# Gated cross-attention block on one core: input norm two batches ahead, gate and up products one step earlier, final sum ahead of a clip, six whole feed-forward row blocks

## The chip, the cores and the metric

The kernel runs on one core of a Trainium2 chip. The metric is the device time of one execution in microseconds. It is written in Bass: every engine has its own instruction stream in program order, and engines wait for each other by semaphores. The engines are TensorE (PE), VectorE (DVE), ScalarE (ACT), GpSimd (POOL), and SyncE (SP), whose queue issues most DMA transfers.

## The reference, cut to what matters

32 batches; per batch x is 100 x 256, the context 1444 x 256, 16 heads of 16, and a hidden width of 704.

```python
h = layernorm(x)                               # "input norm"
q, k, v = h @ Wq.T + bq, ctx @ Wk.T + bk, ctx @ Wv.T + bv
probs = softmax(where(mask, clip(q @ k.T / 4, -50, 50), -10000 -> -50))
delta = layernorm(rs * ((probs @ v) @ Wo.T + bo)) * gamma + beta
x1 = x + tanh(g_xattn) * delta
z = layernorm(x1)                              # then quantised per row to 8 bits
hid = silu(z @ w1.T) * (z @ w2.T)              # gate and up products, ternary weights
out = x1 + tanh(g_ffn) * (quant(hid) @ w3.T)   # "final sum"
```

## The kernel before, in words

Each batch's 1444 context rows are cut into 12 tiles of 121 rows (the last 113) and 3 chunks of 4 tiles. Three batches are in work at once. While the scores and exponentials of batch b run through their 12 steps (n = 0 to 11), the same loop body also does the k and v projections and the input norm and query of batch b+1 (called `c` in the code), the output projection, second norm and gate and up products of batch b-1 (`d`), and the hidden row's quantisation, the down product and the final sum of batch b-2. The order on every engine is written out by hand: each engine has a function `batch` with one `for n in range(NT)` and `if n == ...` lines. Nothing is scheduled by a tool.

In a step TensorE does: 4 score products (`scores`, L1192), half a projection item (`ctx_item`: 3 products of L1233 for k, or 6 of L1247 for v), whatever small product the step has, 4 more score products and the other half item. At n = 1, 5 and 9 it also does the probability times v products of four tiles (`pv`, L1212, 128 records). ScalarE takes each half tile of scores through the exponential (L549, 24 in a batch), copies projections out of PSUM (L561, L570) and copies the results of the small products. VectorE clips each exponentiated tile (`clip`, L783), splits the context into a high and a low part (`split_head` L744, `split_rest` L750), makes the low part of k (`k_rest`, L774), and does the softmax division and both norms. GpSimd makes the small reciprocal roots of the norms and issues the 12 transfers of the stacked query (`stack_q`, L475). SP issues three times 12 transfers of stacked k (`stack_k`, L305) in a batch, and the loads.

The places that the change and the prediction touch:

- All small products share one PSUM bank, `mb`, so each must be read out before the next is written. The output projection (`delta`, L1280, in step 3) writes `mb` after the down product (`down`, L1313, in step 2) has been read by the final sum (`result`, L957 on VectorE), and so it waits for `result_done`:

```python
def delta(b, older):
    pe.wait_ge(dve_post, D_V.after(b, "oT"))
    if older:
        pe.wait_ge(result_done, b.n)
```

- The other waits of TensorE on VectorE that are spoken of: `v_item` (L1247) waits for `k_rest` of the item whose PSUM bank it takes over (`k_lo_done`), `pv` waits for `clip_done`, `x_turn` (L1264) for `xn` and `dl`, `h_turn` (L1306) for `hq`. `scores` waits for the exponential two half tiles before, and at the start of a chunk for its 12 stacked transfers.
- VectorE's steps 1 to 3 before: `split_head`, `k_rest`, `clip`, `split_rest`, `attention_read` and `sums_inverse` (L844 to L855); then `k_rest`, `attention_out`, `clip`, `result`, `x_stats`; then `x_aggr`, `clip`, `x_norm`, `delta_out` (L869). In step 0 it ends the hidden row of batch b-2: `hidden_gate` (L925), `clip`, `hidden_up` (L931), `h_max` (L935), `h_scale`, `h_round`, `h_quant`.
- The input norm is `x_stats`, `x_aggr` (VectorE), `x_rstd_of` (GpSimd, L431 and L433) and `x_norm` (VectorE, L803, waits for GpSimd).
- The gate and up products (`up`, L1298) come in halves of 352 columns: gate 0 and up 0 in step 9, gate 1 in step 10, up 1 in step 11. ScalarE reads each gate half twice (`ffn_gate`, L617 and L618) and each up half once (`ffn_up`, L623).
- The hidden row of 704 is turned in six blocks (`h_turn`), five of 128 columns and one of 64, and read by two activations (`h_turned`, L610 and L611).

A second pass over all batches with `base` set, which guards against infinities, follows under a condition that these inputs don't meet; it is in the program and doesn't run.

Of the kernel before, what the change touches and what calls it, by code (L numbers as in the profile page):

```python
# [41 lines left out]
def flamingo_block(nc, x, ctxT, maskT, g_xattn, g_ffn, wqT, bq, wkT, bk, wvT, bv, woT, bo,  # L42
# [25 lines left out]
    P = 128  # L68
# [37 lines left out]
    with es:  # L106
# [69 lines left out]
        hq = sb("hq", [S, F], bf16)  # L176
# [54 lines left out]
        D_A = Steps("x2T", "t0", "g0", "u0", "t1", "g1", "u1", "hTa", "hTb")  # L231
# [166 lines left out]
        def _(pool):  # L398

            nc.gpsimd.memset(e_sb[2][:, (FT - 1) * H:FT * H], 0.0)  # L400
            nc.gpsimd.memset(e_sb[3][0:TT, (NT - 1) * NB:NT * NB], 0.0).then_inc(s_setp, 1)
# [78 lines left out]
            def batch(b, nxt, prev):  # L480
                for n in range(NT):
                    if n == 3:
                        if nxt:
                            x_rstd_of(b.plus(1))
                            mask_of(b.plus(1))
# [8 lines left out]
                    if n == 11 and nxt:  # L494
                        residual(b.plus(1), prev)

# [19 lines left out]
            def passes(base):  # L516
# [4 lines left out]
                residual(whole(0, base), False)  # L521
                batch(whole(0, base), True, False)
                if base:
                    with pool.Fori(base // 2, (base + NB - 2) // 2) as i:
                        batch(Batch(2 * i + 1, i, 1, base), True, True)
                        batch(Batch(2 * i + 2, i + 1, 0, base), True, True)
                else:
                    for n in range(1, NB - 1):
                        batch(whole(n), True, True)
                batch(whole(NB - 1, base), False, True)  # L530
# [8 lines left out]
        def _(act):  # L539
# [67 lines left out]
            def h_turned(b):  # L607
                act.wait_ge(pe_post, D_T.after(b, "hT"))
                v = mb16[:, 0:FT * S].rearrange("p (k s) -> p k s", k=FT)
                nc.scalar.activation(hT[:, 0:FT - 1, :], v[:, 0:FT - 1, :], ACT.Copy).then_inc(act_post, 1)  # L610
                nc.scalar.activation(hT[0:FL, FT - 1, :], v[0:FL, FT - 1, :], ACT.Copy).then_inc(act_post, 1)  # L611
# [66 lines left out]
        def _(dve):  # L678
# [268 lines left out]
            def h_quant(b):  # L947
                d_wait(b, "hround")
                dv(V.tensor_scalar(hq[:, :], th[:, :], MAGIC, QMAX, ALU.subtract, ALU.min))
# [17 lines left out]
            def batch(b, nxt, prev, prev2):  # L967
# [3 lines left out]
                for n in range(NT):  # L971
# [483 lines left out]
```

## Time and profile before

| | us |
|---|---|
| median of 3 runs (lowest, highest) | 1438.97 (1438.78, 1439.39) |
| the profiled execution's own time | 1438.62 |
| its span, first to last instruction | 1436.8 |
| busy: PE, DVE, ACT, POOL | 1348.5, 1131.2, 965.1, 469.7 |
| busy share: PE, DVE, ACT, POOL | 94%, 79%, 67%, 33% |
| chain that ended last: PE, DVE, ACT, issue | 52%, 25%, 13%, 7% |

The span has three parts: a start of some 70 us (weights, and the projections of the first batch), 31 batches that follow each other in the loop, and an end of some 40 us in which the last batches' remaining work runs one thing after another. Small waits repeat once in each batch, so a wait of half a microsecond stands for some 15 us of the time. "Idle before" of an engine says what ended the idle time; a weight load (PEld) runs ahead of its product, so a wait shows on PEld, on PE, or on both.

### The profile page before, as it was taken

The page shows a single profiled execution, that of the slowest core. Times are in us where ns is not written, and L with a number is a line of the kernel's source. Part 1 is how long each engine was busy: PE and PEld are TensorE (multiplying, and loading weights), DVE is VectorE, ACT ScalarE, POOL GpSimd, SP SyncE. Part 2 cuts the span into 40 slices and gives each one's busy share as a digit, 9 for nine tenths or more (in the row PEclk, how much of TensorE's full clock was granted, in tenths as well). Part 3 has the DMA queues.
Part 4 walks back from the last instruction along what each step waited for, and adds up shares of the span by engine and source line. Part 5 has one row for each costly group of instructions (what it writes and reads, how often), then busy time and mean ns, then how long its engine had stood idle before and what let it go on. Part 6 is the DMA issues. An engine that isn't in the chain of part 4 may idle for free.

```text
span 1436.8 us, 48034 instructions
## 1 busy us (share of the span) xinstructions
PE 1348.5 (94%) x19984; PEld 1220.3 (85%) x19984; DVE 1131.2 (79%) x2241; ACT 965.1 (67%) x1634; POOL 469.7 (33%) x759
## 2 busy tenths in 40 slices
PE   5699999999999999999999999999999999999982
PEld 5599888888988888898888898888889888888971
DVE  6668788878878887877887887888788788878763
ACT  2367776676776767777676777767777767676751
POOL 3523333233333223233323333332333332232310
PEclk9699999999999999999999999999999999999995
DMA  7467666666766666776667676666667666766620
GB/s 217 110 160 174 157 153 156 164 158 167 169 163 155 154 163 166 168 169 156 156 152 171 161 176 160 158 150 161 163 162 173 158 157 155 167 163 162 139 52 8
DMA packets 142477, 222.13 MB, mean 155 GB/s; under 512 B 29162, under 2 KB 135598, under 8 KB 142254
## 3 DMA queue, kind: packets, MB, share of 16 engines
q1 hardware_dynamic: 129966, 199.31, 57.7%
q0 software_dynamic: 12288, 19.69, 6.2%
q8 instruction: 160, 2.62, 0.8%
q14 instruction: 63, 0.52, 0.1%
HBM read 54.00 MB, written 3.28 MB: 40 GB/s over the span
## 4 chain that ended last, share of the span: by engine, by line
PE 52%; DVE 25%; ACT 13%; issue 7%; POOL 2%; SPq 1%; DMA 0%; DVEq 0%; POOLq 0%; ACTq 0%
PE pvb L1212 13%; PE sc L1192 12%; PE cb L1233 11%; PE cb L1247 9%; ACT e_sb L549 7%; DVE e_sb L783 4%; DVE zt L855 3%; DVE c_lo L750 2%; PE mb L1280 2%; PE mb L1271 2%; DVE tiny L935 2%; PE mb L1298 2%; DVE k_lo L774 2%; DVE th L945 1%; ACT us L623 1%
## 5 line engine op out<-in xcount | busy, mean ns | idle before, releaser
L549 ACT ACTIVATE e_sb<-sc 121x800 f32<-121x800 f32 (+1 forms) x768 | 644.8, 844 | 201.4 <-PE sc L1192 191.3
L1192 PE MATMUL sc<-q_st,k_st 96*121 96x200 f32 (+1 forms) x3072 | 476.4, 278 | 7.1 <-DMA q_st<-bd_hi 3.1
L1192 PEld LDWEIGHTS sc<-q_st,k_st 96*121 96x121 f32 (+1 forms) x3072 | 416.3, 186 | 42.5 <-issue 9.0
L783 DVE TENSOR_SCALAR e_sb<-e_sb,hi_b 121x1600 f32<-121x1600 f32 (+1 forms) x384 | 399.4, 1047 | 38.3 <-ACT e_sb L549 38.1
L1212 PE MATMUL pvb<-e_sb,v_sb 121*32 121x100 f32 x12288 | 286.2, 251 | 0.1
L1212 PEld LDWEIGHTS pvb<-e_sb,v_sb 121*32 121x32 f32 x12288 | 264.7, 110 | 22.6 <-issue 19.0
L774 DVE SCALAR_TENSOR_TENSOR k_lo<-cb,bk_c,k_hi 128x484 fp32r<-128x484 f32 (+1 forms) x192 | 134.4, 700 | 137.8 <-ACT k_hi L561 137.8
L1247 PE MATMUL cb<-wv_hi,c_hi 128*121 128x256 f32 (+1 forms) x768 | 227.8, 297 | 15.2 <-DVE k_lo L774 12.2
L475 POOL DMA_DIRECT2D q_st<-bd_hi x256 | 183.2, 719 | 107.9 <-DVE bd_lo L829 104.7
L1247 PE MATMUL cb<-wv_hi,c_lo 128*121 128x256 f32 (+1 forms) x768 | 217.0, 283 | 0.0
L1247 PE MATMUL cb<-wv_lo,c_hi 128*121 128x256 f32 (+1 forms) x768 | 216.9, 282 | 0.0
L431 POOL TENSOR_SCALAR x_ve<-mv 100x1 f32<-100x1 f32 x32 | 24.9, 777 | 560.1 <-DVE mv L799 560.1
L1247 PEld LDWEIGHTS cb<-wv_hi,c_hi 128*121 128x121 f32 (+1 forms) x768 | 142.3, 185 | 26.0 <-DVE k_lo L774 25.2
L1233 PE MATMUL cb<-c_hi,wk_hi 128*128 128x484 f32 (+1 forms) x384 | 154.1, 401 | 0.0
L1233 PE MATMUL cb<-c_hi,wk_lo 128*128 128x484 f32 (+1 forms) x384 | 147.2, 383 | 0.0
L1233 PE MATMUL cb<-c_lo,wk_hi 128*128 128x484 f32 (+1 forms) x384 | 147.0, 383 | 0.0
L1247 PEld LDWEIGHTS cb<-wv_hi,c_lo 128*121 128x121 f32 (+1 forms) x768 | 141.8, 185 | 0.1
L1247 PEld LDWEIGHTS cb<-wv_lo,c_hi 128*121 128x121 f32 (+1 forms) x768 | 141.0, 184 | 0.0
L561 ACT ACTIVATE k_hi<-cb,bk_c 128x484 fp32r<-128x484 f32 (+1 forms) x192 | 126.3, 658 | 4.8 <-PE cb L1233 4.8
L750 DVE TENSOR_TENSOR c_lo<-c_in,c_hi 128x968 fp32r<-128x968 f32 (+1 forms) x96 | 112.4, 1171 | 0.0
L570 ACT ACTIVATE v_sb<-cb 121x512 f32<-121x512 f32 x160 | 97.1, 607 | 21.0 <-PE cb L1247 21.0
L623 ACT ACTIVATE us<-mb,tiny 100x352 f32<-100x352 f32 x64 | 36.6, 572 | 78.0 <-PE mb L1298 78.0
(139 smaller groups left out, 1609.0 us busy)
## 6 DMA issues: line engine op xcount, KB each, us to landing
k_st<-k_hi SPq DMA_DIRECT2D x512, 121.0 KB, 2.8
c_in<-in_ctxT SPq DMA_DIRECT2D x64, 484.0 KB, 3.8
k_st<-k_lo SPq DMA_DIRECT2D x256, 121.0 KB, 2.9
k_st<-k_hi SPq DMA_DIRECT2D x256, 119.0 KB, 2.3
c_in<-in_ctxT SPq DMA_DIRECT2D x32, 476.0 KB, 3.6
k_st<-k_lo SPq DMA_DIRECT2D x128, 119.0 KB, 2.4
q_st<-bd_hi POOLq DMA_DIRECT2D x256, 50.0 KB, 3.3
q_st<-bd_lo POOLq DMA_DIRECT2D x128, 50.0 KB, 3.2
```

What stands on the lines that cost most here:

```text
L475: nc.gpsimd.dma_start(q_st[b.par][QR * part:QR * (part + 1), :, j, :].bitcast(f32), src[QR * j:QR * (j + 1), :, :, :].rearrange("p k a s - ...
L549: nc.scalar.activation(e_sb[e_slot(b, n)][0:TL[n], k * SW:(k + 1) * SW].rearrange("p (o c) -> p o c", o=2), sc[q % NSC][0:TL[n], :, 0:2 * PW],
L561: nc.scalar.activation(k_hi[slot][:, o, 0:CL[u]], cb[o][:, 0:CL[u]], ACT.Identity, bias=bk_c[:, o:o + 1]).then_inc(k_hi_done, 1)
L570: nc.scalar.activation(v_sb[0:TL[n], n:n + 2, :, 0:4:3, :].rearrange("p n q a d -> p (n q) a d"), cb[i][0:TL[n], :].rearrange("p (q a d) - ...
L623: nc.scalar.activation(us[:, cols], mb[0:S, 0:FH], ACT.Copy, scale=tiny[:, 5:6]).then_inc(act_post, 1)
L750: V.tensor_tensor(c_lo[slot][:, :, 0:w], c_in[slot][:, :, 0:w], c_hi[slot][:, :, 0:w].bitcast(f32), ALU.subtract).then_inc(split_done, 1)
L774: V.scalar_tensor_tensor(k_lo[slot][:, o, 0:w], cb[o][:, 0:w], bk_c[:, o:o + 1], k_hi[slot][:, o, 0:w].bitcast(f32), ALU.add, ALU.subtract ...
L783: V.tensor_scalar(e, e, E_LO, hi_b[b.par][0:TL[n], n:n + 1], ALU.max, ALU.min).then_inc(clip_done, 1)
L1192: last = T_.matmul(sc[q % NSC][0:TL[n], e // 2, (e % 2) * PW:(e % 2 + 1) * PW], k_st[st_slot(b, n // TPC)][:, pr // NQ, pr % NQ, t0:t0 + T ...
L1212: last = T_.matmul(pvb[QR * j:QR * (j + 1), col:col + S], v_sb[0:TL[n], n, pr, 2 * a:2 * a + 2, :].rearrange("p x d -> p (x d)"), e[0:TL[n ...
L1233: last = T_.matmul(cb[o][:, 0:w], wt[:, k, o * P:(o + 1) * P], ct[slot][:, k, 0:w], start=i == 0, stop=i == 5)
L1247: last = T_.matmul(cb[i][0:TL[n], half * H:(half + 1) * H], ct[slot][:, k, t0:t0 + TL[n]], wt[:, k, :], start=(k == 0 and a == 0), stop=(k ...
```

## The change

1. **Input norm two batches ahead.** `x_stats` and `x_aggr` of batch b+2 stand at the end of step 9 of batch b, `x_norm` at the head of step 11, and GpSimd's `x_rstd_of(b+2)` at its step 11 behind `stack_q` and `residual`; before they were for batch b+1 in steps 2 and 3. The second batch's norm is made before the loop starts. `split_rest` of the first chunk moves from step 1 to step 2, behind the clip.
2. **Gate and up products one step to the front.** Gate 0 in step 8, up 0 and gate 1 in step 9 (ahead of and behind `pv`), up 1 in step 10; the reads on ScalarE and VectorE move with them, and `h_max` stands at the end of step 11, where it was in step 0 of the next batch.
3. **Final sum ahead of a clip.** `result` stands before the clip in step 2.
4. **Six whole blocks.** `hq` is widened to 768 columns, the last 64 set to zero once, so that `h_turn`, `h_turned` and `down` treat six blocks of 128, and one activation reads them.

```diff
-        hq = sb("hq", [S, F], bf16)
+        hq = sb("hq", [S, FT * P], bf16)
@@ GpSimd, setup and batch
+            nc.gpsimd.memset(hq[:, F:FT * P], 0.0)
...
                     if n == 3:
                         if nxt:
-                            x_rstd_of(b.plus(1))
                             mask_of(b.plus(1))
...
                     if n == 11 and nxt:
                         residual(b.plus(1), prev)
+                        if nxt2:
+                            x_rstd_of(b.plus(2))
@@ ScalarE
-                nc.scalar.activation(hT[:, 0:FT - 1, :], v[:, 0:FT - 1, :], ACT.Copy).then_inc(act_post, 1)
-                nc.scalar.activation(hT[0:FL, FT - 1, :], v[0:FL, FT - 1, :], ACT.Copy).then_inc(act_post, 1)
+                nc.scalar.activation(hT[:, :, :], mb16[:, 0:FT * S].rearrange("p (k s) -> p k s", k=FT), ACT.Copy
+                                     ).then_inc(act_post, 1)
...
-                    if prev and n in (9, 10):
-                        ffn_gate(d, n - 9)
-                    if prev and n in (9, 11):
-                        ffn_up(d, (n - 9) // 2)
+                        ffn_up(d, n - 9)
+                    if prev and n in (8, 9):
+                        ffn_gate(d, n - 8)
@@ VectorE, batch
-                    if nxt:
-                        if n == 3:
-                            x_aggr(c)
-                        if n == 6:
-                            q_head(c)
-                    if prev2 and n == 0:
-                        hidden_gate(b.plus(-2), 1)
+                    if nxt and n == 6:
+                        q_head(c)
                     if prev:
                         if n == 2:
                             attention_out(d)
-                        if n == 10:
-                            hidden_gate(d, 0)
+                        if n in (9, 10):
+                            hidden_gate(d, n - 9)
+                    if nxt2 and n == 11:
+                        x_norm(b.plus(2))
+                    if prev2 and n == 2:
+                        result(b.plus(-2))
                     if n:
                         clip(b, n - 1)
...
-                    if nxt and n % 4 == 1:
+                    if nxt and n in (2, 5, 9):
                         split_rest(c, n // 4)
...
                     if prev2 and n == 0:
-                        hidden_up(b.plus(-2), 1)
-                        for step in (h_max, h_scale, h_round, h_quant):
+                        for step in (h_scale, h_round, h_quant):
                             step(b.plus(-2))
-                    if prev2 and n == 2:
-                        result(b.plus(-2))
-                    if nxt and n == 2:
-                        x_stats(c)
-                    if nxt and n == 3:
-                        x_norm(c)
+                    if nxt2 and n == 9:
+                        x_stats(b.plus(2))
+                        x_aggr(b.plus(2))
...
-                        if n == 10:
-                            hidden_up(d, 0)
+                        if n in (9, 10):
+                            hidden_up(d, n - 9)
+                        if n == 11:
+                            h_max(d)
@@ TensorE, batch
+                        if n == 8:
+                            up(d, 0, 0)
                         if n in (9, 10):
-                            up(d, n - 9, 0)
-                        if n == 11:
-                            up(d, 1, 1)
+                            up(d, n - 9, 1)
                     attend()
...
                     if prev and n == 9:
-                        up(d, 0, 1)
+                        up(d, 1, 0)
```

How the order moves, at three places. First VectorE in steps 1 to 3. The names: `e_sb` is a tile of exponentials, `oT` and `zt` the attention output and the row sums, `y_out` the final sum, `mb` the shared PSUM bank. Before:

```order
L783 TENSOR_SCALAR e_sb<-e_sb,hi_b 121x1600
L750 TENSOR_TENSOR c_lo<-c_in,c_hi 128x968
L844 TENSOR_SCALAR oT<-pvb,submask 128x200
...
L855 RECIPROCAL zt<-zt 128x200
L774 SCALAR_TENSOR_TENSOR k_lo,watch<-cb,bk_c,k_hi 128x476
L859 TENSOR_TENSOR oT<-oT,zt 128x200
L783 TENSOR_SCALAR e_sb<-e_sb,hi_b 121x1600
L957 SCALAR_TENSOR_TENSOR y_out<-mb,tiny,x 100x256
L794 BN_STATS stat<-x_in 100x6
```

With the change:

```order
L787 TENSOR_SCALAR e_sb<-e_sb,hi_b 121x1600
L848 TENSOR_SCALAR oT<-pvb,submask 128x200
...
L859 RECIPROCAL zt<-zt 128x200
L778 SCALAR_TENSOR_TENSOR k_lo,watch<-cb,bk_c,k_hi 128x476
L863 TENSOR_TENSOR oT<-oT,zt 128x200
L961 SCALAR_TENSOR_TENSOR y_out<-mb,tiny,x 100x256
L787 TENSOR_SCALAR e_sb<-e_sb,hi_b 121x1600
L754 TENSOR_TENSOR c_lo<-c_in,c_hi 128x968
```

The low part of the context no longer stands between the clip and the reading of the attention sums, the final sum stands ahead of the second clip, and the input norm's statistics are gone from here.

Second TensorE in steps 8 and 9 (`w12q` are the gate and up weights). Before:

```order
L1233 MATMUL cb<-c_hi,wk_lo 128x484
L1298 MATMUL mb<-w12q,x2T 100x352 x2
L1212 MATMUL pvb<-e_sb,v_sb 32x100 x64
L1298 MATMUL mb<-w12q,x2T 100x352 x2
L1192 MATMUL sc<-q_st,k_st 121x200 x4
```

With the change:

```order
L1237 MATMUL cb<-c_hi,wk_lo 128x484
L1302 MATMUL mb<-w12q,x2T 100x352 x2
L1196 MATMUL sc<-q_st,k_st 121x200 x4
...
L1302 MATMUL mb<-w12q,x2T 100x352 x2
L1216 MATMUL pvb<-e_sb,v_sb 32x100 x64
L1302 MATMUL mb<-w12q,x2T 100x352 x2
L1196 MATMUL sc<-q_st,k_st 121x200 x4
```

The pairs ahead of and behind the `pv` products are now up 0 and gate 1; gate 0 stands a step ahead of them, step 10 has up 1, and step 11 has none.

Third VectorE in steps 9 to 0 (`th`, `gs` and `us` are the hidden row's halves, `stat` and `mv` the input norm's statistics). Before:

```order
L750 TENSOR_TENSOR c_lo<-c_in,c_hi 128x2x476
L774 SCALAR_TENSOR_TENSOR k_lo,watch<-cb,bk_c,k_hi 128x484
L925 SCALAR_TENSOR_TENSOR th<-th,gs 100x352
L783 TENSOR_SCALAR e_sb<-e_sb,hi_b 121x1600
L931 TENSOR_TENSOR gs<-th,us 100x352
L783 TENSOR_SCALAR e_sb<-e_sb,hi_b 121x1600
L925 SCALAR_TENSOR_TENSOR th<-th,gs 100x352
L783 TENSOR_SCALAR e_sb<-e_sb,hi_b 113x1600
L931 TENSOR_TENSOR gs<-th,us 100x352
L935 TENSOR_REDUCE tiny<-gs 100x1
L939 TENSOR_SCALAR tiny<-tiny 100x1
```

With the change:

```order
L754 TENSOR_TENSOR c_lo<-c_in,c_hi 128x2x476
L798 BN_STATS stat<-x_in 100x6
L803 BN_AGGR mv<-stat 100x2
L935 TENSOR_TENSOR gs<-th,us 100x352
L778 SCALAR_TENSOR_TENSOR k_lo,watch<-cb,bk_c,k_hi 128x484
L929 SCALAR_TENSOR_TENSOR th<-th,gs 100x352
L787 TENSOR_SCALAR e_sb<-e_sb,hi_b 121x1600
L935 TENSOR_TENSOR gs<-th,us 100x352
L807 TENSOR_SCALAR xn<-x_in,mv,x_rstd 100x256
L787 TENSOR_SCALAR e_sb<-e_sb,hi_b 121x1600
L939 TENSOR_REDUCE tiny<-gs 100x1
L787 TENSOR_SCALAR e_sb<-e_sb,hi_b 113x1600
```

The hidden row's second half and its maximum come ahead of the clip of tile 11, and `xn`, which waits for GpSimd, now has the clips of tiles 10 and 11 behind it. On GpSimd the order of the instructions is the same as before (`x_res`, `x_ve`, `x_rstd`, `hi_b`, `d_ve`); only the batch whose norm they make is one later.

## Rows read from the trace of the kernel before

**Rows 1.** The page, its first line.
```profile
span 1436.8 us, 48034 instructions
```

**Rows 2.** Windows of two batches: us; PE, PEld, DVE, ACT, POOL busy; PEclk, DMA, GB/s.
```profile
91.30:131.64 40.34, 39.79 (x614) 36.55 (x613) 31.35 (x61) 29.35 (x50) 13.63 (x23) 1.00 0.71 171
723.34:765.53 42.19, 41.28 (x626) 37.58 (x625) 34.41 (x69) 29.99 (x52) 13.99 (x23) 1.00 0.68 157
```

**Rows 3.** Who waited for whom, whole run: engine, line, releaser; us, times, longest.
```profile
PEld mb L1280 <- issue: 26.9, 29, 0.9
...
PE mb L1280 <- DVE y_out L957: 21.7, 29, 0.8
...
PEld cb L1247 <- DVE k_lo L774: 25.2, 58, 9.9
...
PE mb L1306 <- DVE hq L949: 6.4, 2, 3.7
```

**Rows 4.** Chain of waits from 734 to 740 us: start, us, what.
```profile
735.41 0.96 DVE e_sb L783
...
736.38 0.41 DVE y_out L957
```

**Rows 5.** Timeline of TensorE, same batch: start, us, engine, line, operation, count, idle before.
```profile
726.67 2.96 PE L1212 MATMUL pvb<-e_sb,v_sb 121*32 121x100 f32 x128
...
732.36 0.95 PE L1313 MATMUL mb<-w3q,hT 128*100 128x256 bf16 x6
...
735.88 0.28 PE L1247 MATMUL cb<-wv_lo,c_hi 128*121 128x256 f32 x1
...
736.92 1.08 PE L1280 MATMUL mb<-wo,oT 128*100 128x256 f32 x4 [0.75 <-DVE y_out L957]
```

**Rows 6.** Timeline of VectorE, same batch.
```profile
725.45 0.89 DVE L935 TENSOR_REDUCE tiny<-gs 100x1 f32<-100x704 f32 x1
...
730.11 1.16 DVE L750 TENSOR_TENSOR c_lo<-c_in,c_hi 128x968 fp32r<-128x968 f32 x1
...
731.18 0.42 DVE L844 TENSOR_SCALAR oT<-pvb,submask 128x200 f32<-128x200 f32 x1
...
734.51 0.62 DVE L774 SCALAR_TENSOR_TENSOR k_lo<-cb,bk_c,k_hi 128x476 fp32r<-128x476 f32 x1
...
736.29 0.48 DVE L957 SCALAR_TENSOR_TENSOR y_out<-mb,tiny,x 100x256 f32<-100x256 f32 x1
...
739.46 0.42 DVE L869 SCALAR_TENSOR_TENSOR dl<-mb,bo_t 100x256 f32<-100x256 f32 x1
...
749.57 0.72 DVE L774 SCALAR_TENSOR_TENSOR k_lo<-cb,bk_c,k_hi 128x484 fp32r<-128x484 f32 x1
```

**Rows 7.** Timeline of ScalarE, same batch, steps 10 and 11.
```profile
762.87 0.84 ACT L549 ACTIVATE e_sb<-sc 121x800 f32<-121x800 f32 x1
...
764.78 0.59 ACT L623 ACTIVATE us<-mb,tiny 100x352 f32<-100x352 f32 x1
```

**Rows 8.** Timeline of GpSimd, same batch.
```profile
760.56 0.75 POOL L439 TENSOR_TENSOR x_res<-x_in,beta_t 100x256 f32<-100x256 f32 x1
```

**Rows 9.** Groups by line and shape, GpSimd: busy us, mean ns, idle before.
```profile
L446 POOL TENSOR_SCALAR d_ve<-dmv,scal 100x1 f32<-100x1 f32 x32 | 43.9, 1371 | 97.2 <-DVE dmv L879 97.2
```

**Rows 10.** Timeline of the SP queue, same batch, with the landing of such a transfer.
```profile
751.98 1.99 SPq L305 DMA_DIRECT2D k_st<-k_hi  x2
...
762.17 0.70 SPq L305 DMA_DIRECT2D k_st<-k_lo  x1
```

**Rows 11.** The page, DMA issues: count, KB each, median us to landing.
```profile
k_st<-k_lo SPq DMA_DIRECT2D x256, 121.0 KB, 2.9
```

**Rows 12.** Timeline of VectorE, start and end of the run.
```profile
57.53 1.05 DVE L783 TENSOR_SCALAR e_sb<-e_sb,hi_b 121x1600 f32<-121x1600 f32 x1 [6.52 <-ACT e_sb L549]
...
1395.70 0.52 DVE L925 SCALAR_TENSOR_TENSOR th<-th,gs 100x352 f32<-100x352 f32 x1
...
1397.80 0.15 DVE L939 TENSOR_SCALAR tiny<-tiny 100x1 f32<-100x1 f32 x1
```

More of the change, by code:

```diff
@@ L478, in stack_q, with batch @@
                         ).then_inc(q_stacked[b.par], 16)
-            def batch(b, nxt, prev):
+            def batch(b, nxt, prev, nxt2=True):
                 for n in range(NT):
@@ L521, in passes @@
                 residual(whole(0, base), False)
+                x_rstd_of(whole(1, base))
                 batch(whole(0, base), True, False)
                 if base:
-                    with pool.Fori(base // 2, (base + NB - 2) // 2) as i:
+                    with pool.Fori(base // 2, (base + NB - 4) // 2) as i:
                         batch(Batch(2 * i + 1, i, 1, base), True, True)
                         batch(Batch(2 * i + 2, i + 1, 0, base), True, True)
+                    batch(whole(NB - 3, base), True, True)
                 else:
-                    for n in range(1, NB - 1):
+                    for n in range(1, NB - 2):
                         batch(whole(n), True, True)
-                batch(whole(NB - 1, base), False, True)
+                batch(whole(NB - 2, base), True, True, False)
+                batch(whole(NB - 1, base), False, True, False)
                 delta_rstd(whole(NB - 1, base))
@@ L965, in result, with batch @@
                     y.then_inc(result_done, 1)
-            def batch(b, nxt, prev, prev2):
+            def batch(b, nxt, prev, prev2, nxt2=True):
                 own = prev
@@ L1123, in passes @@
                         v_guard(b, u, 1)
+                x_stats(whole(1, base))
+                x_aggr(whole(1, base))
+                x_norm(whole(1, base))
                 batch(whole(0, base), True, False, False)
@@ L1127, in passes @@
                 if base:
-                    with dve.Fori(base // 2 + 1, (base + NB - 2) // 2) as i:
+                    with dve.Fori(base // 2 + 1, (base + NB - 4) // 2) as i:
                         batch(Batch(2 * i + 1, i, 1, base), True, True, True)
                         batch(Batch(2 * i + 2, i + 1, 0, base), True, True, True)
+                    batch(whole(NB - 3, base), True, True, True)
                 else:
-                    for n in range(3, NB - 1):
+                    for n in range(3, NB - 2):
                         batch(whole(n), True, True, True)
+                batch(whole(NB - 2, base), True, True, True, False)
                 e = whole(NB - 1, base)
-                batch(e, False, True, True)
+                batch(e, False, True, True, False)
                 clip(e, NT - 1)
-                hidden_gate(e.plus(-1), 1)
-                hidden_up(e.plus(-1), 1)
-                for step in (h_max, h_scale, h_round, h_quant, result):
+                for step in (h_scale, h_round, h_quant, result):
                     step(e.plus(-1))
@@ L1304, in h_turn @@
                 for k in range(FT):
-                    m = P if k < FT - 1 else FL
-                    last = T_.transpose(mb16[0:m, k * S:(k + 1) * S], hq[:, k * P:k * P + m], identb[0:S, 0:S])
+                    last = T_.transpose(mb16[:, k * S:(k + 1) * S], hq[:, k * P:(k + 1) * P], identb[0:S, 0:S])
                 last.then_inc(pe_post, 1)
             def down(b):
-                pe.wait_ge(act_post, D_A.after(b, "hTb"))
+                pe.wait_ge(act_post, D_A.after(b, "hT"))
                 for k in range(FT):
-                    m = P if k < FT - 1 else FL
-                    last = T_.matmul(mb[0:S, 0:H], hT[0:m, k, :], w3q[0:m, k, :], start=k == 0, stop=k == FT - 1)
+                    last = T_.matmul(mb[0:S, 0:H], hT[:, k, :], w3q[:, k, :], start=k == 0, stop=k == FT - 1)
                 last.then_inc(pe_post, 1)
```

5 lines of the change are left out of this document (2 added, 3 removed).

## The prediction

> **What bounds the kernel now.** I read the page first: the span is 1436.8 us [rows 1], the execution's own time 1438.62, so 1.8 lie around the span, and the median of the runs is 0.35 above that execution. TensorE is 94% busy in the table, the others at most 79%, so what counts is what TensorE does or waits for. Next I cut out one batch of the loop, the seventeenth, from its first score product to the first of the next: 42.19 us at the full granted clock, 2.4 GHz, of which TensorE is busy 41.28, VectorE 34.41, ScalarE 29.99 [rows 2]. The second batch, which has no down product and no final sum in it, takes 40.34. Third, the list of waits. Only three of TensorE's waits repeat in each batch [rows 3]: the output projection L1280 waits for the final sum L957, 29 times, 0.93 us each on the weight loads (26.9) and 0.75 on the products; and L1247 waits for the low part of k, L774. Of the latter's 25.2 us one wait is 9.9 and belongs to the start; the other 57, about two in a batch, hold 15.3. The weight loads lose more than the products show, because a product's modelled end runs on into the wait: from the last L1247 at 735.88 to L1280 at 736.92 are 1.04 us start to start [rows 5]. I take the 0.93. Last, the chain of waits around that place reads: clip 0.96 us, final sum 0.41, then L1280 [rows 4]. So VectorE's order there sets when TensorE goes on. All else in the loop is TensorE's own work.
>
> Below, clock times are those of this batch, and "would" times are on the same clock, with nothing saved earlier.
>
> **Final sum ahead of the clip.** VectorE's queue can be walked along its timeline [rows 6], beside TensorE's [rows 5]. The four-tile `pv` product ends at 726.67 + 2.96 = 729.63, but VectorE begins to read it at 731.18, 1.55 later, since it is still at older work. Of that work the change takes away the split of the context (1.16, at 730.11), the maximum of the hidden row (0.89, at 725.45) and the last product ahead of it; it puts x_norm (under 0.5, as the 100x256 operation at 739.46) and the maximum ahead of tile 11's clip, so that this clip is later by some 0.45 and what follows it earlier by more than 1.55. The reading is then bound by `pv` and begins at about 729.65. The shuffle and the reciprocal take what they take now, 734.51 - 731.18 = 3.33, so L774 begins at 733.0 instead of 734.51 and the final sum, without the clip's 0.96 ahead of it, at 733.0 + (736.29 - 734.51) - 0.96 = 733.8. Its input, the down product, is there at 732.36 + 0.95 = 733.3 [rows 5]. It ends at 734.2, while TensorE, rid of the wait for L774 too, wants the bank at 735.7. Margin 1.5 us, so the whole wait goes: **-26.9 us**. What waits instead: the clip of tile 1, now behind the final sum (it ends at 735.2), is wanted by `pv` in step 5, several us later. Late next would be TensorE's own work.
>
> **Less ahead of the low part of k.** The first wait of the pair is in step 2: L774 ends at 733.6 instead of 735.1, wanted at about 734.9. The second is in step 6. The output projection's result is read by L869 at 739.46; in the change final sum (0.4), clip, split (1.07) and clip put it at 733.8 + 0.4 + 0.96 + 1.07 + 0.96 = 737.2, and the projection, begun at 735.7, ends at 735.7 + 1.08 = 736.8. VectorE's chain from there through both norms' small steps keeps its length, so L774 at 749.57 would come 2.2 earlier, while TensorE comes only 1.2 earlier: no wait. **-15.3 us**. If the waits stay as they are, this is 0; that is the other bound.
>
> **The end of the run.** The last execution of `hidden_gate`, `hidden_up` and `h_max` for batch 30 stands bare between 1395.70 and 1397.80 [rows 12], with TensorE waiting for `hq` behind it (L1306 waited twice, 6.4 us in all [rows 3]). The change has done it by then, in a stretch where VectorE has idle time: **-2.1 us**. The last batch's feed-forward is serial as before.
>
> **Edits I cost at nothing.** Gate and up products: the same four pairs in the same batch, one step earlier; cover is that TensorE never waits for them now. ScalarE reads them by 1 us (gate) and 0.6 (up, 764.78 [rows 7]); with gate 0 read in step 8, its exponentials of steps 9 and 10 come some 0.5 later, e.g. 763.4 for the one at 762.87, and end at 764.3. Score products want the exponential two half tiles back, the next such at about 764.7, so 0.3 to 0.5 us of margin is left. If it is gone, 0.3 a batch is 9 us. Six whole blocks: as many products as before, one activation in place of two; some 0.1 us of ScalarE, covered by its idle 12 us a batch [rows 2]; the memset once. Norm two ahead: VectorE's 1 us a batch moves to steps 9 and 11, where it waits for ScalarE anyway. Split one step later: its output, at 736.2, is first wanted in step 4, behind the rest of step 3 (14 products, an estimate of 2 us from 735.7 + 1.1 on). SP is held by it too, since the load behind it waits; the store and the 12 transfers of stacked k stand behind that load, but these wait for TensorE's step 3 anyway. At the start, the second batch's norm stands before the first clip, which follows 6.52 us of idle time [rows 12]: 0, at most 2.
>
> **GpSimd**, of which VectorE now waits at x_norm with two clips behind it. It ends the batch's twelve query transfers and the residual at 760.56 + 0.75 = 761.3 [rows 8]. Its two small norm operations are bounded by the costliest such row, 1.37 us each [rows 9], so the root is there by 764.2 at the latest; VectorE comes to x_norm at about 764.4, since it first waits for up 1 from ScalarE. No wait, by little at the upper bound and by over 1 us otherwise.
> A 100x1 operation of 1.37 us [rows 9] did not compute for that long: it stood behind something. The Trainium skill, page "SBUF — State Buffer", section "Who interferes with whom", says that a VectorE instruction in a two-port mode, which tensor_scalar can enter, holds the port pair that it shares with GpSimd to its end, and GpSimd blocks fully. By that rule each clip that meets these two operations or a query transfer adds up to a clip's length to them; that is the slower rival below, and the sum above holds with the bound of the row.
>
> **The sum.** 1438.62 - 26.9 - 15.3 - 2.1 = 1394.3, and 0.35 more on the scale of the median: with half of it, **1394.5 us**. A batch would take 42.19 - 0.93 - 0.5 = 40.8.
>
> **The rivals.**
> - *Stacked k is late.* The twelve transfers of chunk 0 are issued from 751.98, the last at 762.17 [rows 10], and such a one lands 2.9 us later [rows 11]: 765.1, with the next batch's first score at 765.53. 0.5 us is all. TensorE's stretch from step 7 to there has no wait to lose, so it doesn't get shorter, which speaks against this; for it speaks that the DMA share, 0.68, rises with each shorter batch. At 0.5 a batch over 30 batches: 1409.5. Chance 0.13.
> - *The waits for the low part of k stay*, because ScalarE's high part comes as late as ever: 1438.6 - 26.9 - 2.1 = 1409.6. Chance 0.08.
> - *ScalarE is short in steps 9 to 11*, 0.3 a batch: 1403. Chance 0.07.
> - *GpSimd stops VectorE*, the one that ends slower. If the root comes L after 764.4, clips 10 and 11 come L later. Tile 11's clip would end at about 767.5, and TensorE wants it some 3.5 later at `pv`; beyond 3.5, each us costs TensorE one. From L = 4.9 on the saving of 1.4 a batch is eaten. That needs GpSimd to be ready only at 769.3, five to six clips of lockout more than the row's bound. At L = 6: 1394.5 + 30 x 2.5 = 1469.5. Chance 0.03.
> - *It doesn't do what it says*: VectorE comes to the final sum before the down product is out, waits there with the clips behind it, and TensorE waits for those. The margin is 0.5 us and the clips aren't wanted for longer. Within 0.2% of before; chance 0.02.
>
> **The numbers.** The forecast itself has 0.67. 0.2%, 2.9 us, is about what a measurement can tell from no change. Faster by more: 0.67 + 0.13 + 0.08 + 0.07 = 0.95, of which I keep 0.94; within it 0.02; slower 0.04. The range runs from 1389 (5 us more, if the waits' starts hide some and the end gains at a better clock) to 1410, which takes in the first three rivals.
>
> **What would show it.** Right: L1280's wait for L957 gone from the list, a batch of 40.8, L774 with a wait or two at the start alone, L957 ahead of a clip at once behind L859. Wrong: a wait of VectorE at L807 for GpSimd, of L1196 for k_st or for e_sb some 30 times, or a batch over 41.3.

## The result, and the profile after

The changed kernel takes **1372.43 us** (median of four runs, 1371.17 to 1372.54); the kernel before, timed beside it, takes 1439.18 (1438.78 to 1439.76). The ratio is 0.9534, with a 95% interval from 0.9517 to 0.955. The forecast was 1394.5 with a range from 1389 to 1410: the direction held, but the time lies 17 us under the range. In the profiled executions the span went from 1436.8 [rows 1] to 1370.8, by 66.0; the walk had accounted for 44.3.

The page after: its first line, the busy times, and the chain that ended last:

```profile
span 1370.8 us, 48003 instructions
...
PE 1310.4 (96%) x19984; PEld 1211.7 (88%) x19984; DVE 1124.0 (82%) x2241; ACT 961.6 (70%) x1602; POOL 457.0 (33%) x760
...
PE 87%; SPq 4%; DVE 3%; DMA 2%; POOL 2%; ACT 1%; issue 1%; DVEq 0%; POOLq 0%; ACTq 0%
```

Next the windows. In both kernels the third batch begins at 131.7; the last begins at 1356.9 before and at 1295.6 after. First before, then after (columns as in [rows 2]), the latter with the partner of the second batch in [rows 2]:

```profile
131.70:1356.90 1225.20, 1197.54 (x18099) 1090.05 (x18098) 998.50 (x2001) 870.59 (x1480) 405.78 (x667) 1.00 0.68 161
```

```profile
131.70:1295.60 1163.90, 1161.82 (x18098) 1081.71 (x18097) 991.33 (x2000) 867.33 (x1451) 392.81 (x665) 1.00 0.72 170
693.30:733.30 40.00, 40.00 (x626) 37.31 (x625) 34.19 (x70) 29.89 (x51) 13.48 (x23) 1.00 0.72 170
```

These 29 batches lost 1225.2 - 1163.9 = 61.3 us, the end of the run 79.9 - 75.2 = 4.7, the start nothing. The two columns to compare are the length and PE's busy time. TensorE's idle time fell from 27.7 to 2.1, but its busy time fell too, by 35.7 us, although it does the same number of products (18099 and 18098). So the loop got shorter by more than its listed waits.

Now TensorE's waits over the whole run (answers to [rows 3]):

```profile
PE mb L1268 <- DVE xn L807: 13.7, 1, 13.7
PE cb L1251 <- DVE k_lo L778: 9.7, 2, 9.5
...
PE mb L1309 <- DVE hq L953: 3.7, 1, 3.7
...
PE sc L1196 <- DMA k_st<-k_lo: 2.0, 6, 0.7
```

No wait for the final sum (L961 now) is left, and those for `k_lo` are the one of the start and a short one. No wait of TensorE for VectorE repeats in each batch any more. Last, the same place in the same batch. TensorE and VectorE, to be laid beside [rows 5] and [rows 6], whose clock is 30.04 us later (first scores at 723.34 before, 693.30 after):

```profile
699.53 0.44 PE L1309 MATMUL mb<-identb,hq 100*128 100x100 bf16 x6
699.78 0.65 PE L1196 MATMUL sc<-q_st,k_st 96*121 96x200 f32 x4
...
702.08 0.82 PE L1315 MATMUL mb<-w3q,hT 128*100 128x256 bf16 x6
702.65 0.65 PE L1196 MATMUL sc<-q_st,k_st 96*121 96x200 f32 x4
...
703.87 0.58 PE L1196 MATMUL sc<-q_st,k_st 96*121 96x200 f32 x4
704.28 0.29 PE L1251 MATMUL cb<-wv_hi,c_hi 128*121 128x256 f32 x1
704.41 0.28 PE L1251 MATMUL cb<-wv_hi,c_lo 128*121 128x256 f32 x1
...
704.88 0.28 PE L1251 MATMUL cb<-wv_lo,c_hi 128*121 128x256 f32 x1
705.00 1.03 PE L1284 MATMUL mb<-wo,oT 128*100 128x256 f32 x4
```

```profile
699.66 0.42 DVE L848 TENSOR_SCALAR oT<-pvb,submask 128x200 f32<-128x200 f32 x1 [0.48 <-PE pvb L1216]
...
703.00 0.61 DVE L778 SCALAR_TENSOR_TENSOR k_lo<-cb,bk_c,k_hi 128x476 fp32r<-128x476 f32 x1
...
703.54 0.36 DVE L863 TENSOR_TENSOR oT<-oT,zt 128x200 f32<-128x200 f32 x1
703.82 0.48 DVE L961 SCALAR_TENSOR_TENSOR y_out<-mb,tiny,x 100x256 f32<-100x256 f32 x1
704.21 1.04 DVE L787 TENSOR_SCALAR e_sb<-e_sb,hi_b 121x1600 f32<-121x1600 f32 x1
```

And the rows of before that stand between those of [rows 5]:

```profile
729.56 0.56 PE L1306 MATMUL mb<-identb,hq 100*128 100x100 bf16 x6
730.05 0.67 PE L1192 MATMUL sc<-q_st,k_st 96*121 96x200 f32 x4
...
733.24 0.67 PE L1192 MATMUL sc<-q_st,k_st 96*121 96x200 f32 x4
...
734.48 0.57 PE L1192 MATMUL sc<-q_st,k_st 96*121 96x200 f32 x4
735.19 0.38 PE L1247 MATMUL cb<-wv_hi,c_hi 128*121 128x256 f32 x1
735.41 0.28 PE L1247 MATMUL cb<-wv_hi,c_lo 128*121 128x256 f32 x1
```

Read them start to start, since ends are modelled and busy time hides what follows. Four differences make up the batch:
- *L1280's wait.* From the last value product to the output projection: 1.04 before, 0.12 after (704.88 to 705.00), **0.92**.
- *The wait for the low part of k.* Scores to value product 0.71 against 0.41, and that product to the next 0.22 against 0.13: 0.39 here. At the other place in the batch, step 6, both together are 0.81 before (749.76 to 750.57) and 0.58 after (717.74 to 718.32), 0.23: in all **0.62**.
- *The turn.* From its first transpose to the next scores 0.49 before (729.56 to 730.05), 0.25 after: **0.24**.
- *The down product.* To the next scores 0.88 before (732.36 to 733.24), 0.57 after: **0.31**.

Together 2.09 of the 2.19 us by which this batch got shorter (42.19 to 40.00). The last two, 0.55 in all, were in no term of the prediction. The other batches after are like this one, but for seven that are 0.4 to 0.7 longer, mostly at a score product of TensorE that waits for stacked k.

### The profile page after: what moved, and what is told of

Read it like the earlier page. It is cut to its first block, busy times and chain, and to the rows that moved or that the text cites. A ratio compares the mean times of both kernels' runs of the same rounds, so it can differ in the third digit from the quotient of the medians.

```text
span 1370.8 us, 48003 instructions
## 1 busy us (share of the span) xinstructions
PE 1310.4 (96%) x19984; PEld 1211.7 (88%) x19984; DVE 1124.0 (82%) x2241; ACT 961.6 (70%) x1602; POOL 457.0 (33%) x760
## 4 chain that ended last, share of the span: by engine, by line
PE 87%; SPq 4%; DVE 3%; DMA 2%; POOL 2%; ACT 1%; issue 1%; DVEq 0%; POOLq 0%; ACTq 0%
PE sc L1196 22%; PE pvb L1216 19%; PE cb L1251 18%; PE cb L1237 17%; SPq L305 4%; PE mb L1302 3%; PE mb L1275 2%; PE mb L1284 2%; DMA k_st<-k_lo 2%; PE mb L1315 2%; PE mb L1309 1%; POOL q_st L476 0%; PE mb L1268 0%; ACT e_sb L554 0%; POOL e_sb L514 0%
## 5 line engine op out<-in xcount | busy, mean ns | idle before, releaser
L1251 PE MATMUL cb<-wv_hi,c_hi 128*121 128x256 f32 (+1 forms) x768 | 222.3, 289 | 9.9 <-DVE k_lo L778 9.7
L476 POOL DMA_DIRECT2D q_st<-bd_hi x256 | 164.6, 647 | 115.9 <-DVE bd_lo L833 113.1
L447 POOL TENSOR_SCALAR d_ve<-dmv,scal 100x1 f32<-100x1 f32 x32 | 43.9, 1373 | 433.4 <-DVE dmv L883 433.4
L476 POOL DMA_DIRECT2D q_st<-bd_lo x128 | 91.3, 713 | 0.1
```

Source lines behind the costliest of these rows:

```text
L476: nc.gpsimd.dma_start(q_st[b.par][QR * part:QR * (part + 1), :, j, :].bitcast(f32), src[QR * j:QR * (j + 1), :, :, :].rearrange("p k a s - ...
L1251: last = T_.matmul(cb[i][0:TL[n], half * H:(half + 1) * H], ct[slot][:, k, t0:t0 + TL[n]], wt[:, k, :], start=(k == 0 and a == 0), stop=(k ...
```

## Experiments

The first theory, A, said that the narrow sixth block cost TensorE those 0.55 us a batch. Twelve kernels were run. Ten take parts of the change away, apply them without the rest, or change one size; e11 adds work that nothing uses, and e12 tries a better start.

### The six whole blocks

**e1**: before, with the blocks whole and nothing else (four functions as in the change's diff: `hq` of six blocks, one activation, no `m` in `h_turn` and `down`).

> The kernel before with only the six whole blocks of 128. Theory A (the last, 64-wide block holds up TensorE itself, at the turn of the hidden row and at the down product): between the traces before and after, TensorE's start-to-start times around these 12 products fall by about 0.53 us a batch (0.23 at the turn, 0.30 at the down product), over 31 loop batches 16 us; but before, the output projection waits for the final sum, and the final sum for VectorE, not for TensorE, so behind the turn and the down product (steps 1 and 2) TensorE would arrive at that wait earlier and wait longer: 1439 less 0 to 3 us, with L1280's wait grown from 0.93 to about 1.4 us. Theory A without that cover: 1423. Theory B (the blocks cost nothing, as forecast, and the surplus comes from the other edits together): within 1 us of 1439, L1280's wait as it was, and the start-to-start times around the last block still long.

Measured: 1444.48 us (1442.66 to 1447.79), ratio 1.0036 (1.0022 to 1.005): slower by 5.6, which neither theory had. No saving shows, and seven batches of the trace are some 1.3 us longer than the others (the profiled execution is the slowest of the five, 1447.79). One of them, in windows:

```profile
780.33:783.39 3.06, 1.54 (x12) 1.18 (x11) 3.06 (x7) 1.53 (x3) 0.00 (x0) 1.00 0.70 194
783.39:786.61 3.22, 3.22 (x11) 2.70 (x12) 2.27 (x7) 0.42 (x1) 1.54 (x3) 0.50 0.11 32
```

and TensorE's timeline in it:

```profile
781.66 0.38 PE L1247 MATMUL cb<-wv_hi,c_hi 128*121 128x256 f32 x1 [0.76 <-DVE k_lo L774]
...
783.39 1.98 PE L1280 MATMUL mb<-wo,oT 128*100 128x256 f32 x4 [0.77 <-DVE y_out L957]
```

The narrow blocks' time came off, as in the change, but TensorE then came earlier to waits that end no earlier: the one for `k_lo` grew to 0.76, that for the final sum stayed. After this half-idle stretch the granted clock was 0.50 (1.2 GHz) for some 3.2 us. A batch without such a fall takes 42.2, as before. The one that begins at 727.58 has almost the same two waits (0.71 and 0.76) and no fall; what decides between them no run shows.

**e2**: the change without the blocks (its other parts kept).

> The changed kernel with the 64-wide last block back and two activations. Theory A: nothing waits in the loop of the changed kernel, so the 0.53 us a batch shows in full: 1372.4 + 16 = 1388. Theory B: 1372 to 1373.

Measured: 1388.97 us, ratio 0.9654 (0.9638 to 0.967), 16.5 above the change. That is Theory A's number. A batch is 40.5, against 40.0. So the blocks' 0.55 us are worth everything where TensorE is the bound, and nothing where it waits.

**e9 and e10** ask what the cost hangs on. e9 makes the sixth block 96 wide (`FW` is 96), not full, but wider than 64:

```diff
-                    last = T_.transpose(mb16[:, k * S:(k + 1) * S], hq[:, k * P:(k + 1) * P], identb[0:S, 0:S])
+                    m = P if k < FT - 1 else FW
+                    last = T_.transpose(mb16[0:m, k * S:(k + 1) * S], hq[:, k * P:k * P + m], identb[0:S, 0:S])
```

and the same `m` in `down`, the activation in two again.

> The changed kernel with its sixth feed-forward block 96 wide instead of 128, in the turn and in the down product (64 wide in the kernel before). Theory: TensorE pays for a block of 64 rows or fewer because it changes its way of working there; a block of 96 does not count as narrow, so nothing comes back: 1372 to 1374 us. Rival: any block that is not full costs, so the 16.5 us that the whole blocks were worth in e2 come back: about 1389 us.

Measured: 1370.48 us, ratio 0.9522 (0.9506 to 0.9538), an interval that overlaps the change's (0.9517 to 0.955). A block of 96 costs nothing, and nor do the two activations that this kernel has again.

e10 gives the down product alone its block of 64 back:

```diff
-                    last = T_.matmul(mb[0:S, 0:H], hT[:, k, :], w3q[:, k, :], start=k == 0, stop=k == FT - 1)
+                    m = P if k < FT - 1 else FL
+                    last = T_.matmul(mb[0:S, 0:H], hT[0:m, k, :], w3q[0:m, k, :], start=k == 0, stop=k == FT - 1)
```

> The changed kernel with the last block of the down product alone 64 rows deep again; the turn keeps six whole blocks. Theory: in e2's trace the down product with the narrow block was 0.30 us of a batch longer up to the next score product, the turn 0.23: 0.30 x 31 = 9 us, so 1381 to 1382 us. Rivals: the turn's output shape alone mattered, 1372 us; the down product alone mattered, 1389 us.

Measured: 1381.04 us, ratio 0.9597 (0.9581 to 0.9613), 8.6 above the change. In its trace the turn is short and the down product long:

```profile
703.01 0.44 PE L1309 MATMUL mb<-identb,hq 100*128 100x100 bf16 x6
703.27 0.65 PE L1196 MATMUL sc<-q_st,k_st 96*121 96x200 f32 x4
...
705.57 0.95 PE L1316 MATMUL mb<-w3q,hT 128*100 128x256 bf16 x6
706.44 0.67 PE L1196 MATMUL sc<-q_st,k_st 96*121 96x200 f32 x4
```

0.87 from 705.57 to 706.44, where the change has 0.57: 0.30 x 31 = 9.3. Both places cost by themselves: 8.6 us come back with the down product, and the 7.9 that are missing to e2 are the turn's by difference. Of the two widths that were run, 64 costs and 96 doesn't. The Trainium skill, page "TensorEngine Tiling (Array Packing)", section "Tiling Modes", says that changing the tiling mode "drains the TensorE", and lists modes for 64 rows or columns but none for 96. The runs agree with it; that the drain is what takes the time was not measured by itself.

**e11** tests the clock in e1: eight products that nothing uses, put into TensorE's wait for the final sum.

```diff
+                if older and not b.base:
+                    for _i in range(8):
+                        T_.matmul(cb[1][:, 256:384], identb[:, :], identb[:, :], start=True, stop=True)
                 if older:
                     pe.wait_ge(result_done, b.n)
```

> e1 (the kernel before with the six whole blocks alone) and in each batch eight further 128x128 products ahead of the wait for the final sum, about 0.4 us of work in a wait of 0.9 us; their output is used by nothing. Theory: e1 lost because TensorE, done earlier, waited longer and its granted clock fell to half (1.2 GHz) eight times in the loop; with the filler the falls go, and the time is at or under that of the kernel before, 1437 to 1440 us, with the granted clock at 0.97 or more. Rival: the falls have nothing to do with the length of that wait, or the filler lies on the path: 1444 us or more (1444 + 31 x 0.4 = 1456 if all of it lies on the path).

Measured: 1438.74 us, ratio 0.9998 (0.9989 to 1.0008), 5.7 under e1 with more work in it. The windows from 300 to 1290 us, e11 first, e1 second:

```profile
300.00:1290.00 990.00, 967.01 (x14782) 888.48 (x14782) 808.57 (x1623) 701.94 (x1171) 323.70 (x533) 1.00 0.69 162
```

```profile
300.00:1290.00 990.00, 955.76 (x14544) 879.65 (x14543) 802.89 (x1605) 697.97 (x1163) 320.64 (x529) 0.99 0.68 161
```

With the filler the falls of the loop are gone (1.00; there were seven in e1, not eight), and the time is that of before: the filler lies in the wait. So e1's loss was the clock, and its missing gain lies in the waits.

### The wait for the final sum

**e3**: before, with `result` ahead of the clip in step 2, nothing else.

```diff
+                    if prev2 and n == 2:
+                        result(b.plus(-2))
                     if n:
                         clip(b, n - 1)
...
-                    if prev2 and n == 2:
-                        result(b.plus(-2))
```

> The kernel before with only the final sum moved ahead of the clip in step 2. My walk along VectorE's queue: the final sum would begin 0.96 us earlier, at 735.33 on the clock of the seventeenth batch, end at 735.7, and TensorE wants the bank at 736.0: the wait of 0.93 us goes nearly whole, 1439 - 27 = 1412, perhaps 1 to 3 us less of it. Rival (the wait only shrinks by part, since a semaphore and the product's own start lie between): 0.3 us a batch stay, 1421. The waits for the low part of k stay in both.

Measured: 1439.0 us, ratio 1.0 (0.999 to 1.001). A clear miss for the walk, by which this edit alone was the largest term. The wait for L957 is gone from the list, but the batch is 42.2 as before. TensorE's timeline:

```profile
736.71 1.05 PE L1280 MATMUL mb<-wo,oT 128*100 128x256 f32 x4
...
740.77 0.36 PE L1264 MATMUL mb<-identf,xn 100*128 100x100 f32 x2 [0.80 <-DVE dl L869]
```

and its VectorE:

```profile
736.05 0.48 DVE L957 SCALAR_TENSOR_TENSOR y_out<-mb,tiny,x 100x256 f32<-100x256 f32 x1
736.45 1.05 DVE L783 TENSOR_SCALAR e_sb<-e_sb,hi_b 121x1600 f32<-121x1600 f32 x1
...
739.87 0.42 DVE L803 TENSOR_SCALAR xn<-x_in,mv,x_rstd 100x256 f32<-100x256 f32 x1 [0.77 <-POOL x_rstd L433]
740.20 0.42 DVE L869 SCALAR_TENSOR_TENSOR dl<-mb,bo_t 100x256 f32<-100x256 f32 x1
```

The output projection starts without a wait, and 0.8 us are lost four microseconds later, at the next user of the bank `mb`, which waits until L869 has read the projection. L869 starts 740.20 - 724.07 = 16.13 us into the batch; before it was 739.46 - 723.34 = 16.12 [rows 2, 6]. Swapping two operations of VectorE left the end of its queue where it was.

From this came the second theory, Q: what bounds the batch of before is one stretch of VectorE's queue, from tile 11's clip to L869, and a part of the change is worth what it takes out of that stretch; the place of the wait on TensorE only shows where it comes out.

**e4**: the change, with `result` behind the clip again (the reverse of e3's diff).

> The changed kernel with the final sum behind the clip again. By my walk VectorE comes to it 1.55 us earlier than before through the other edits, so that it would end at about 735.2 on that clock, with TensorE there at 735.7 less the 0.5 that the whole blocks save it: the margin is near 0, and 0 to 0.3 us a batch are lost: 1372 to 1382. Rival (the place of the final sum alone decides): the whole wait of 0.93 us is back, 1372.4 + 27 = 1399.

Measured: 1385.45 us, ratio 0.9632 (0.9616 to 0.9648), 13.0 above the change, between the two expectations. The weight loads' waits say why:

```profile
PEld mb L1284 <- issue: 12.8, 30, 0.4
```

Of the 0.9 us of before, 0.4 come back, since VectorE now reaches the clip earlier.

**e5 to e8**: the gate and up products alone (e5) and left out (e8), and the norm with the final sum alone (e6) and the norm left out (e7). e5 is before with the products a step earlier (`up`, `ffn_gate`, `ffn_up`, `hidden_gate`, `hidden_up`, `h_max` as in the change); e6 is before with the norm two ahead and `result` ahead of the clip; e7 is the change with the norm of before; e8 the change with the products' steps of before. The edits are the change's own lines, here VectorE's of e8:

```diff
+                    if prev2 and n == 0:
+                        hidden_gate(b.plus(-2), 1)
...
-                        for step in (h_scale, h_round, h_quant):
+                        hidden_up(b.plus(-2), 1)
+                        for step in (h_max, h_scale, h_round, h_quant):
```

> The kernel before with only the gate and up products (and their reads and the maximum) one step to the front. Theory Q, formed after the final sum alone gave nothing (its wait went to the transpose of the normed input, L1264, which waits for L869): the loop waits on one queue, VectorE's work from the clip of tile 11 to L869, and a cut shortens a batch only by what it takes out ahead of the wait that comes last. This edit takes the second hidden_up (0.56) and the maximum (0.92) from between tile 11's clip and the reading of the attention sums, and puts 0.2 us before the clip: all of L774, L957 and L869 come about 1.25 us earlier, within the 1.55 at which pv binds. 1439 - 30 x 1.25 = 1401, L1280's wait for L957 gone or under 0.3. Rival (my forecast: this edit costs and gives nothing by itself): 1439.

> The kernel before with the input norm two batches ahead and the final sum ahead of the clip, nothing else. Theory Q: the final sum alone moved the wait to L1264; with statistics, norm and the wait for GpSimd (1.7 us together) out of the way L869 comes 1.7 earlier, so the 0.93 is now really gained, and the 0.2 of L774 in step 6 too; the 0.5 in step 2 stays. 1439 - 30 x 1.1 = 1406. Rival (VectorE's total work is what counts, and the norm only moves it): 1439, with the wait at another place.

> The changed kernel with the input norm of the next batch in steps 2 and 3 again. Theory Q: the reading of the attention sums is bound by pv, the rest of the queue to L869 is 1.7 to 1.9 us longer, and TensorE stands at L1264 for nearly all of it: 1372 + 30 x 1.8 = 1426. Rival (the parts' gains add, and the norm's is the third or so that is left): 1390.

> The changed kernel with gate and up products, their reads and the maximum where they were before. Theory Q: 1.5 us come back into the queue ahead of the reading of the attention sums, but the split is gone from there (1.07), so the reading is only some 0.45 us later than pv allows; L957 and L869 still come about when TensorE wants them. 0 to 0.3 us a batch and the 2 us at the end: 1374 to 1383. Rival (this edit's part of the gain is as large as alone): 1372 + 38 = 1410.

Measured:

| kernel | time us | ratio (interval) | batch us | L869/L873 into the batch |
|---|---|---|---|---|
| before | 1438.84 | | 42.19 | 16.12 |
| e3, final sum | 1439.0 | 1.0 (0.999 to 1.001) | 42.21 | 16.13 |
| e7, without norm | 1428.69 | 0.9933 (0.9916 to 0.9949) | 41.80 | 15.74 |
| e6, norm and final sum | 1401.19 | 0.9739 (0.9723 to 0.9755) | 40.94 | 14.30 |
| e5, products | 1398.62 | 0.9723 (0.9707 to 0.9739) | 40.92 | 14.84 |
| e8, without products | 1384.54 | 0.9623 (0.9607 to 0.9639) | 40.37 | 14.30 |
| the change | 1372.43 | 0.9534 (0.9517 to 0.955) | 39.99 | 13.92 |

The last two columns are taken from starts in the traces, for the nineteenth batch. All four came within 5 us of Q, and the rivals of e7 (1390) and e8 (1410) are out. In before, e3, e5, e7 and e8 the next batch begins 26.05 to 26.08 us after the start of L869 (L873), wherever that is: there VectorE's stretch is the bound. It runs on through both norms to the low part of k in step 6, which comes 10.11 us behind L869 before (739.46 to 749.57) and 10.12 behind L873 in the change (707.21 to 717.33). e6 has 26.64: its stretch is short enough for 14.30 + 26.07 = 40.4, but its narrow blocks and its waits for `k_lo` hold TensorE longer. In the change both bounds meet: VectorE's is 13.92 + 26.07 = 39.99, and TensorE's own work is 40.00 without a wait. In e7, which has the final sum ahead, the products and the blocks, but not the norm, 56 of the 67 us of gain are missing. The wait stands at the transpose of the normed input, which wants `xn` and a bank that L869 has read (weight loads of e7):

```profile
PEld mb L1261 <- DVE xn L803: 53.1, 30, 2.1
```

No run moved the split of the context by itself (e5 and e6 leave it in step 1, e7 and e8 keep it in step 2), so its share is not known.

### A better start

**e12**. In the trace of the change the first exponential comes at 56.81 us. VectorE, GpSimd and ScalarE before it:

```profile
35.58 10.79 DVE L1098 TENSOR_SCALAR e_sb<-e_sb,wscale 128x1408 f32<-128x1408 f32 x2
...
35.53 5.41 POOL L514 TENSOR_SCALAR e_sb<-e_sb 128x1536 f32<-128x1536 f32 x1
41.02 4.60 POOL L516 TENSOR_SCALAR w3q<-e_sb 128x1536 bf16<-128x1536 f32 x1
...
56.81 1.57 ACT L554 ACTIVATE e_sb<-sc 121x800 f32<-121x800 f32 x2 [4.67 <-PE sc L1196]
```

VectorE's two steps take 6.11 and 4.76 us, and end 0.75 us behind one of GpSimd's each (at 41.69 behind 35.53 + 5.41 = 40.94, and at 46.37 behind 41.02 + 4.60 = 45.62). e12 lets GpSimd stack the first queries without waiting for the weights' scales, and gives the down weights' three steps to VectorE (the later two edited alike):

```diff
-            w3s = e_sb[2][:, 0:FT * H]
-            nc.gpsimd.tensor_scalar(w3s, w3s, wscale[:, 2:3], MAGIC, ALU.mult, ALU.add).then_inc(s_setg, 1)
...
+            stack_q(whole(0))
...
-            for i in range(2):
+            for i in range(3):
                 sv(f"w{i + 1}a", V.tensor_scalar(w12s[i], w12s[i], wscale[:, i:i + 1], MAGIC, ALU.mult, ALU.add))
```

> The changed kernel with another start: GpSimd stacks the first batch's queries before it waits for the weights' scales, and the three rounding steps of the down weights move from GpSimd to VectorE, beside those of the gate and up weights. In the trace of the changed kernel the first exponential starts at 56.8 us, behind GpSimd's steps of 5.4 and 4.6 us and beside VectorE's of 6.1 and 4.8, where one such step alone took 0.9. Theory: the steps of the two engines slow each other; apart they are short, and the first exponential starts at 45 to 47 us: 1361 to 1363 us in all. Rival: the start waits for the weights' loads or for TensorE's context items, and the time stays at 1370 to 1373 us.

Measured: **1360.73 us** (1356.96 to 1362.33), ratio 0.945 (0.9434 to 0.9467), 11.7 under the change and faster than both kernels.

```profile
34.03 3.22 DVE L1091 TENSOR_SCALAR e_sb<-e_sb,wscale 128x1408 f32<-128x1408 f32 x3
...
45.72 1.59 ACT L548 ACTIVATE e_sb<-sc 121x800 f32<-121x800 f32 x2 [3.27 <-PE sc L1191]
```

Three steps now take 3.22 us, 1.07 each, and the first exponential starts 11.1 us earlier. How the two edits share this was not run. That the two engines' steps held each other up is what the Trainium skill's page "SBUF — State Buffer", section "Who interferes with whom", says of `tensor_scalar`: the one that issues first holds the port pair for the whole instruction. The rows agree as far as VectorE goes: 6.11 and 4.76 us beside GpSimd's steps, with their ends just behind these, and 1.07 without them. What GpSimd's steps take alone no run shows.

## Why the prediction missed

Point by point:
- **What bounds the kernel**: right only in part. VectorE's order did set TensorE's pace, but the view that "only three of TensorE's waits repeat in each batch" left out time that no list of waits holds. Between the third batch and the last, 61.3 us went, 19.1 more than the 42.2 of the listed waits.
- **"Six whole blocks: as many products as before", costed at nothing**: the step that failed. The count of products was the same, but a block of 64 is not a narrower block at the same price. e2 puts it at 16.5 us, the down product alone at 8.6 (e10). Its place could be timed before the change: 0.49 us for the six transposes and 0.88 for the six products up to the next scores. With 16.5 less, the forecast would have been 1378.0, 5.6 above the measured time.
- **"Final sum ahead of the clip: -26.9"**: the wait did go, VectorE's reading is bound by `pv` (the 0.48 at L848), and the start behind L863 came as walked (703.82 - 693.30 = 10.5 us into the batch, as 733.8 - 723.34). But as the price of this edit it is false: alone it is worth 0 (e3), and left out it costs 13.0 (e4). The time behind the wait is won only where L869 comes earlier too, as with the norm and with the products (e5 to e8). The walk moved all parts at once, and for all together it held: L869 was to come at 737.2, 13.9 us into the batch, and came at 13.91. It never asked what each part was worth, and failed on e3.
- **"Less ahead of the low part of k: -15.3"**: right mechanism, small size. A wait of the list costs its own time and, in step 2, also 0.09 us on the product behind it: 0.62 a batch, 0.62 x 29 = 18.0, so about 3 us more. The margin of 1.0 us in step 6 wasn't there, though. L774 came 2.2 earlier as walked, but TensorE, with the blocks' time off too, came as much earlier (750.35 - 30.04 - 718.15 = 2.16).
- **"The end of the run: -2.1"**: the work is gone from the tail as said. VectorE at the end of the change:

```profile
1331.40 1.05 DVE L787 TENSOR_SCALAR e_sb<-e_sb,hi_b 113x1600 f32<-113x1600 f32 x1
1332.37 0.14 DVE L943 TENSOR_SCALAR tiny<-tiny 100x1 f32<-100x1 f32 x1
```

  From the last batch's start on 4.7 us went, and the sum had 2.1. None of L1280's waits for the final sum stood in that part before. The blocks took some 0.55 of the rest in steps 1 and 2; the remaining 2 were not told apart.
- **"Gate and up products", "Norm two ahead", costed at nothing**: as moves of TensorE's and VectorE's load they were free, but they are what makes the final sum's place pay (e5, e6, e7), and so no small parts.
- **GpSimd**: right for the root of the input norm. VectorE waits for it once, at the start (L807 for L434, 4.4 us), never in the loop, where before it waited 0.8 us a batch (23.5 in 31). But for the second norm's root it waits 1.07 us in each batch, as before (L893 for L452, 34.2 us in 32), while GpSimd's L447, a 100x1 operation of 1.40 us, stands beside a clip. That wait lies in the stretch from L873 to the low part of k, which now is as long as TensorE's work; what it costs was not tested. In the setup, where I hadn't looked, VectorE's two steps beside GpSimd's took some 9 us longer than without them.
- **The rivals**: stacked k late is there in a few batches (2.0 us of waits in six), not in thirty; the four others did not come.

Of the 21.7 us by which the span fell further than the sum, the blocks are 16.5, the low part of k about 3, the end of the run 2; the small rest was not told apart. The low end of the range rested on waits' starts and the clock alone and gave no room to an edit costed at nothing.

## What to carry to other kernels

Price each shape that TensorE runs by start to start up to the next product, not by the count of products: a block of 64 behind five full ones cost 0.24 to 0.31 us here, a padded one nothing. When a wait is to be removed by a swap on the releasing engine, follow that engine's queue to its next output that anyone wants: if the same work is still ahead of that, the wait moves and the time stays. And a saving on the engine that waits is worth nothing until the queue that it waits for is shorter, so test such parts both alone and left out.

## What the runs showed of the hardware

- A saving can make a kernel slower: TensorE came some 0.5 us earlier to its waits, which then were 0.76 and 0.77 us, and in seven batches of the profiled run some 3.2 us at 1.2 GHz followed. The kernel took 5.6 us more (e1); eight products in the wait took that back (e11).
- A transpose or product of 64 as the last of six costs TensorE 0.24 and 0.31 us (e2, e10); one of 96 nothing that can be measured (e9).
- A `tensor_scalar` of VectorE that takes 1.07 us by itself (e12) took 6.11 and 4.76 beside GpSimd's, and ended 0.75 us behind those (the change's trace).
